# Keys and values of one more batch in three fp32r products, and new orders on all engines, in a fused attention and BitLinear kernel

## What is computed

```python
def xattn(q, ctx, mask):
    Q, K, V = proj(q, wq, bq), proj(ctx, wk, bk), proj(ctx, wv, bv)
    scores = jnp.where(mask == 0, 1e-9, Q @ K.T / sqrt(32))
    return softmax(scores) @ V @ wo + bo

def bitlinear(x, w, b):          # rmsnorm, 8-bit rows of x, ternary w
    return act_quant(rmsnorm(x)) @ weight_quant(w).T + b

x = x + xattn(layernorm(x), ctx, mask)
x = x + bitlinear(gelu(bitlinear(layernorm(x), w1, b1)), w2, b2)
```

## Time and profile before

| what | value |
|---|---|
| median of 3 runs | 652.19 us (651.63 to 652.81) |
| the profiled execution | 650.6 us |
| its span in the trace | 648.8 us |
| granted TensorE clock | 1.00 |
| PE busy | 628.9 us (97%) |
| DVE busy | 574.3 us (89%) |
| ACT busy | 530.2 us (82%) |
| POOL busy | 518.7 us (80%) |

### The profile page before, as it was taken

How to read it: one execution, slowest core, us unless ns; L and a number is a source line. 1 busy time by engine, 2 the same in 40 slices (tenths; PEclk the granted TensorE clock), 3 DMA queues, 4 the chain that set the end, 5 groups by cost and what they waited for, 6 DMA issues and landing times.

```text
span 648.8 us, 14114 instructions
## 1 busy us (share of the span) xinstructions
PE 628.9 (97%) x4904; PEld 423.7 (65%) x4904; DVE 574.3 (89%) x1062; ACT 530.2 (82%) x1450; POOL 518.7 (80%) x653
## 2 busy tenths in 40 slices
PE   8988999999999999999999999999999999999996
PEld 6746886666666676766666676666667666565542
DVE  5697889999999988999899988999889799999894
ACT  2579679987889888887898878888988889998674
POOL 3297977979977898688967899778959778999776
PEclk9999999999999999999999999999999999999999
DMA  8983310424315443354224343043333122543236
GB/s 291 402 300 111 126 41 9 107 45 106 84 28 115 103 91 75 38 135 90 71 67 114 74 121 74 10 132 87 90 74 74 24 75 41 128 86 88 62 61 182
DMA packets 109286, 65.38 MB, mean 101 GB/s; under 512 B 90856, under 2 KB 90856, under 8 KB 108576
## 3 DMA queue, kind: packets, MB, share of 16 engines
q1 hardware_dynamic: 108159, 64.49, 37.9%
q10 hardware_dynamic: 1056, 0.00, 0.1%
HBM read 35.12 MB, written 8.39 MB: 67 GB/s over the span
## 4 chain that ended last, share of the span: by engine, by line
PE 67%; POOL 13%; DVE 8%; DMA 4%; ACT 4%; issue 3%; SPq 0%; POOLq 0%; DVEq 0%; ACTq 0%
PE ps_a L573 23%; PE ps_y L710 11%; PE ps_z L687 11%; PE ps_t L646 6%; PE ps_s L636 4%; PE ps_a L658 3%; POOL hid L2270 2%; POOL prob L2259 2%; DMA q_hT<-q_h 2%; PE ps_y L580 2%; DVE hs L1633 2%; POOL q_h L2275 2%; PE ps_a L607 2%; ACT prob L1145 2%; DMA wk_s<-in_L_xattn_wk_dram 1%
## 5 line engine op out<-in xcount | busy, mean ns | idle before, releaser
L1145 ACT ACTIVATE prob<-ps_s,nmax 128x120 f32<-128x120 f32 x512 | 178.9, 377 | 24.7 <-DVE nmax L1579 19.2
L2259 POOL TENSOR_TENSOR prob<-prob,pinv 128x480 f32<-128x480 f32 x128 | 129.2, 1017 | 41.0 <-DVE pinv L1584 40.0
L687 PE MATMUL ps_z<-w1T,q_xT 128*128 128x512 fp8e4 x476 | 122.8, 380 | 0.5 <-DVE hid L1625 0.4
L1145 ACT ACTIVATION_READ_ACCUMULATOR prob<-ps_s,nmax 128x1 f32 x512 | 113.3, 221 | 0.0
L710 PE MATMUL ps_y<-w2T,q_hT 128*128 128x512 fp8e4 x448 | 105.5, 379 | 1.5 <-DMA q_hT<-q_h 1.5
L1625 DVE SCALAR_TENSOR_TENSOR hid<-ps_z,y_deq,b_row 128x512 f32<-128x512 f32 x119 | 88.0, 739 | 10.6 <-PE ps_z L687 9.2
L1576 DVE COPY_PREDICATED_SCALAR ps_s<-hidden_key,masked_c 128x480 f32 x128 | 90.5, 707 | 4.2 <-PE ps_s L636 3.9
L1121 ACT COPY probT<-ps_t 120x512 f32<-120x512 f32 x128 | 76.9, 601 | 15.4 <-PE ps_t L646 14.3
L1579 DVE TENSOR_REDUCE nmax<-ps_s 128x4 f32<-128x480 f32 x128 | 84.1, 657 | 4.4
L646 PE MATMUL ps_t<-ident,prob 128*120 128x128 f32 x512 | 77.9, 275 | 4.3 <-POOL prob L2259 3.7
L646 PEld LDWEIGHTS ps_t<-ident,prob 128*120 128x120 f32 x512 | 60.0, 137 | 25.3 <-issue 7.4
(11 more groups left out here) (207 smaller groups left out, 1373.7 us busy)
## 6 DMA issues: line engine op xcount, KB each, us to landing
x<-in_x_dram SPq DMA_DIRECT2D x32, 256.0 KB, 2.9
out_dram<-x SPq DMA_DIRECT2D x32, 256.0 KB, 2.8
xn<-in_x_dram SPq DMA_DIRECT2D x7, 1024.0 KB, 6.6
hid<-in_L_ffn_w_dram SPq DMA_DIRECT2D x4, 1024.0 KB, 9.6
ctx_k<-in_ctx_dram SPq DMA_DIRECT2D x8, 240.0 KB, 3.1
ctx_k<-in_mask_Bx1xSxS_ik_dram SPq DMA_DIRECT2D x7, 240.0 KB, 3.1
xn<-in_x_dram SPq DMA_DIRECT2D x4, 256.0 KB, 3.5
x<-in_L_xattn_wq_dram SPq DMA_DIRECT2D x1, 1024.0 KB, 7.3
```

The source lines that it names most:

```text
L687: last = nc.tensor.matmul(bank[:], q_xT[:, k % 3, i], w1T[:, i, c * CH:(c + 1) * CH], start=(i == 0), stop=(i == KD - 1))
L1145: last = nc.scalar.activation(prob[:, n % 3, g * S2:(g + 1) * S2], ps_s[n % HG][:, g * S2:(g + 1) * S2], ACT.Exp, bias=nmax[:, n % 4, g:g ...
L2259: gp.tensor_tensor(pr, pr, pinv[:, n % 4].unsqueeze(2).to_broadcast([P, HG, S2]), ALU.mult).then_inc(s["prob_ready"], 1)
```

## The change

One number changes, `CTX3` from 3 to 2, and the lists of all five engines are written out anew. Nothing else differs: the steps themselves, their buffers and their waits are the same text (the waits that name `CTX3` follow it). The diff has 1848 lines; its core, stretch by stretch:

```diff
-    CTX3 = 3
+    CTX3 = 2
...
             load_wk()
+            load_piece(0)
             load_piece(1)
-            load_piece(0)
+            load_piece(2)
             load_piece(3)
-            load_piece(2)
             load_x(1)
+            load_first_mask()
             load_wo()
-            load_first_mask()
             load_wv()
...
+            load_x(2)
+            load_residual(5)
+            load_mask(1)
             load_residual(1)
```

PE, the start, one loop iteration's first part, and the end:

```diff
             turn_xn(0, 2)
+            turn_xn(0, 3)
             project_ctx(0, "k")
-            turn_xn(0, 3)
-            turn_keys(0)
             first_q(0)
             first_q(1)
             first_q(2)
+            turn_keys(0)
...
             for a in range(2, 6):
                 ffn_up(4 * a - 4, 2)
+                turn_probs(16 * a - 3)
                 scores(4 * a)
                 turn_xn(a + 1, 0)
-                turn_probs(16 * a - 3)
                 ffn_up(4 * a - 4, 3)
+                turn_probs(16 * a - 2)
                 project_out(4 * a - 2)
                 turn_xn(a + 1, 1)
+                turn_probs(16 * a - 1)
                 ffn_up(4 * a - 3, 0)
-                turn_probs(16 * a - 2)
                 project_ctx(a + 1, "k")
                 ffn_up(4 * a - 3, 1)
                 ffn_down(4 * a - 5, 0)
-                turn_probs(16 * a - 1)
                 ffn_down(4 * a - 5, 1)
...
             ffn_up(31, 1)
-            ffn_down(28, 0)
             ffn_up(31, 2)
             ffn_up(31, 3)
+            ffn_down(28, 0)
             ffn_down(28, 1)
```

ACT, the start and the roundings (they stood after `evac_probs(18)` and `evac_probs(24)`):

```diff
+            evac_turn(("x", 0, 3))
             evac_keys(0)
-            evac_turn(("x", 0, 3))
-            evac_q(0, 0)
             sum_abs(0)
             sum_abs(2)
+            evac_q(0, 0)
...
             evac_turn(("x", 1, 3))
+            round_wv()
             evac_probs(5)
+            exps(8)
             evac_q(1, 0)
             evac_piece(4, 0)
+            round_wk()
             evac_probs(6)
```

DVE, the start and the new list from the third tile's maxima to the first up product (the splits stood after `oT_low(5)` and `softmax_max(29)`):

```diff
             sum_abs(1)
+            sum_abs(3)
             add_bk(0)
             scale_bq()
-            sum_abs(3)
             weight_scales(0)
             ln1_stats(1, 0)
             ln1_stats(1, 1)
+            hide(0, mask0_in)
             ln1_stats(1, 2)
             ln1_stats(1, 3)
-            hide(0, mask0_in)
```

DVE, one loop iteration's first part, and the end:

```diff
                 evac_up(4 * a - 4, 2)
+                invert_sums(16 * a - 1)
                 softmax_max(16 * a)
+                evac_up(4 * a - 4, 3)
                 softmax_max(16 * a + 1)
-                invert_sums(16 * a - 1)
-                evac_up(4 * a - 4, 3)
...
             evac_up(30, 0)
-            ln2_scales(31)
             evac_up(30, 1)
             evac_up(30, 2)
+            ln2_scales(31)
             evac_up(30, 3)
             h_scale(29)
```

POOL, the start, the stretch of the w2 pieces and the loop's first part:

```diff
             round_piece(1)
+            ln1_apply((0, 1))
             normalize(0)
             round_piece(2)
             normalize(1)
-            ln1_apply((0, 1))
             ln1_apply((2, 3))
...
             add_bo(0)
+            normalize(6)
             round_piece(5)
-            add_bo(1)
-            normalize(6)
+            round_piece(6)
             normalize(7)
-            round_piece(6)
             round_piece(7)
             normalize(8)
+            add_bo(1)
+            round_piece(4)
             normalize(9)
-            round_piece(4)
...
             for a in range(2, 6):
+                normalize(16 * a - 2)
+                round_x(4 * a - 3)
                 y_factor(4 * a - 3)
-                round_x(4 * a - 3)
-                normalize(16 * a - 2)
+                normalize(16 * a - 1)
                 add_bo(4 * a - 1)
```

More of the change, by code:

```diff
@@ L813, in _ @@
             turn_piece(6, (0, 1))
+            project_q(1, 2)
+            scores(3)
+            turn_piece(6, (2, 3))
             turn_probs(9)
-            project_q(1, 2)
-            turn_piece(6, (2, 3))
-            scores(3)
+            project_out(1)
             turn_piece(7, (0, 1))
             turn_probs(10)
-            project_out(1)
             turn_piece(7, (2, 3))
@@ L1018, in _ @@
             attend(26)
+            scores(28)
             ffn_up(24, 2)
             turn_probs(109)
-            scores(28)
+            project_out(26)
             turn_probs(110)
-            project_out(26)
             ffn_up(24, 3)
+            turn_probs(111)
             ffn_down(22, 0)
-            turn_probs(111)
             ffn_up(25, 0)
@@ L1774, in _ @@
             evac_piece(1, 1)
+            evac_piece(1, 3)
             softmax_max(3)
@@ L1885, in _ @@
             ln1_stats(3, 3)
-            evac_down(0)
-            softmax_max(25)
+            residual(4)
+            ln2_stats(4)
+            evac_up(3, 0)
             softmax_max(26)
-            residual(4)
-            evac_up(3, 0)
+            add_bk(2)
             invert_sums(24)
-            add_bk(2)
-            ln2_stats(4)
+            invert_sums(25)
             softmax_max(27)
-            invert_sums(25)
+            h_scale(2)
+            invert_sums(26)
             ln2_scales(4)
-            h_scale(2)
+            evac_up(3, 1)
             hide(2, mask_in)
-            invert_sums(26)
+            oT_low(5)
             softmax_max(28)
-            evac_up(3, 1)
-            oT_low(5)
-            split_wk()
-            evac_down(1)
             invert_sums(27)
@@ L1978, in _ @@
-                invert_sums(16 * a + 9)
+                invert_sums(16 * a + 8)
+                residual(4 * a)
+                invert_sums(16 * a + 9)
+                ln2_stats(4 * a)
+                ln1_stats(a + 2, 3)
+                evac_up(4 * a - 1, 0)
+                softmax_max(16 * a + 10)
                 softmax_max(16 * a + 11)
-                add_bk(a + 1)
-                evac_up(4 * a - 1, 0)
-                ln1_stats(a + 2, 3)
+                ln2_scales(4 * a)
+                hide(a + 1, mask_in)
@@ L2033, in _ @@
             evac_up(21, 3)
+            xT_low(7, 2)
             softmax_max(101)
+            residual(23)
+            evac_up(22, 0)
             invert_sums(99)
-            xT_low(7, 2)
-            residual(23)
             h_scale(21)
+            add_bv(7)
             invert_sums(100)
-            evac_up(22, 0)
-            add_bv(7)
+            ln2_stats(23)
+            evac_up(22, 1)
             xT_low(7, 3)
-            evac_up(22, 1)
-            ln2_stats(23)
             softmax_max(102)
+            softmax_max(103)
+            invert_sums(101)
             oT_low(24)
+            evac_up(22, 2)
+            evac_down(20)
+            invert_sums(102)
             ln2_scales(23)
-            invert_sums(101)
-            softmax_max(103)
-            evac_up(22, 2)
-            invert_sums(102)
-            evac_down(20)
+            invert_sums(103)
             evac_up(22, 3)
-            invert_sums(103)
+            add_bk(7)
             softmax_max(104)
@@ L2112, in _ @@
             softmax_max(118)
+            softmax_max(119)
+            invert_sums(116)
+            evac_up(26, 0)
+            residual(27)
             evac_down(23)
-            evac_up(26, 0)
-            softmax_max(119)
-            residual(27)
-            invert_sums(116)
             ln2_stats(27)
+            evac_up(26, 1)
             invert_sums(117)
```

789 lines of the change are left out of this document (390 added, 399 removed).

## The result

The median went from 651.33 to **655.42 us** (15 runs each, 653.39 to 657.6 after): ratio 1.006, 95% interval 1.0051 to 1.007. That is slower by 0.6%, 4.1 us, inside the predicted range (649.9 to 656.3), but not the likeliest case (652.9, no change) and above the forecast's own range of 651.4 to 654.4. Two single runs, one of before at 908.49 us and one of `late_splits` at 716.77, lie far above the others of their kernel and are left out where kernels are compared. The profiled execution of after took 653.84 us, span 651.8, 3.0 longer than the span of before; its mean granted clock is 0.997.

What follows compares the result with a forecast made beforehand. PE was taken as the bound, busy 628.9 of 648.8 us, with DVE second. Products -1.3, splits +2.4, start +0.4, relief -0.8, loop and tail zero gave +0.7: median 652.9 us, range 649.9 to 656.3.

Steps and rivals of the forecast that it cites:

- the likeliest case: Whole kernel: terms sum to +0.7 us, median 652.9, no change that counts; chance 0.38.
- Products: Third batch on PE: two fp32 products become three fp32r products each, 3.43 to 2.80 us apiece; -1.3 us.
- Splits: wk's and wv's subtractions move to about 65 to 80 us, overfilling DVE; PE loses +2.4 us, bounds 0.9 and 3.5.
- three places that I had named: From 66 to 96: w2 transposition waits for its bank, query product for the residual, ACT for maxima.
- the one slack of 1.1 at 90.89: The evacuation at 89.17 ends 1.1 us before PE needs its bank; this was set against DVE's 3.5 us overrun.
- Start: First weight sums: last piece now summed on DVE, POOL begins 0.5 us later; +0.4 at PE, bounds 0 and 0.8.
- Relief: Where the splits leave, 142 to 165 us, PE's 0.78 us lost should go; -0.8, bounds 0 and -1.85.
- Loop: Four iterations of 74.4 us without a PE gap can only get worse; forward probability transposition has 1.4 us to spare; zero.
- the rival's mechanism: Loop: scaling for the forward probability transposition slips past its 1.4 us, PE waits four times, 1.0 each; 656.9, chance 0.10.
- The sign I had argued: Loop: with no PE gap in its four iterations, it could only get slower, not faster; size taken as zero.
- Tail: After the loop, end set by tile 29; later up product eats into PE's 1.85 us wait; zero, bound 1.0 either way.
- two held-up splits: Both splits collide with POOL from 65 to 89 us: PE loses 3.5, sum +1.8, 654.0; chance 0.20.

Runs made afterwards that it cites:

- late_splits: The changed kernel with the products of the kernel before (CTX3 = 3) and roundings and splits at their old places; 659.84 us, ratio 1.0143.
- new_tail: The kernel before (CTX3 = 3) with only what follows the loop taken from the changed kernel; 652.23 us, ratio 1.0014.
- old_loads: The changed kernel with the old order of the first loads and of the sums that follow them; 653.98 us, ratio 1.0047.
- h_sooner: The changed kernel with the two roundings of a hidden tile one step sooner on POOL in the loop; 652.81 us, ratio 1.0043.
- tail_apart: h_sooner with one POOL bias addition moved ahead of the rounding of tile 27 in the tail; 654.46 us, ratio 1.0052.
- new_loop: The kernel before (CTX3 = 3) with only the loop's new lists from the changed kernel; 653.61 us, ratio 1.0036.

## Why the range held and the likeliest case did not

*Products: right.* The third batch's products stand in the chain of after at 2.78 and 2.80 us.

```profile
119.17 2.78 PE ps_a L573 x12
...
124.12 2.80 PE ps_a L573 x12
```

*Splits: right mechanism, too dear.* DVE's timeline after:

```profile
24.65 2.29 DVE L1690 TENSOR_REDUCE w_abs<-raw_wv_h 128x1 f32<-128x2048 f32 x1 [3.36 <-DMA raw_wv_h<-in_L_ffn_w_dram]
...
67.70 3.30 DVE L1726 TENSOR_TENSOR wv_l<-wv_s,wv_h 128x2048 fp32r<-128x2048 f32 x1
...
77.89 2.26 DVE L1721 TENSOR_TENSOR wk_l<-wk_s,wk_h 128x2048 fp32r<-128x2048 f32 x1
...
100.53 0.65 DVE L1730 TENSOR_TENSOR ctxT_l<-ps_y,ctxT_h 128x480 fp32r<-128x480 f32 x1
```

3.30 + 2.26 = 5.56 against the 5.7 taken: one held up, one free, as in the earlier trace rows. DVE is full, a bank's evacuation is what PE waits for at 82.72, and the residual at 75.23, two of the three places that I had named. But PE loses 1.33 and not 2.4 from 66 to 96 (bounds 0.9 and 3.5). I set DVE's overrun against the one slack of 1.1 at 90.89; PE's largest wait there is 0.69 for POOL, which both splits held up in turn (POOL's timeline):

```profile
68.96 3.81 POOL L2314 TENSOR_SCALAR hid<-hid 128x2048 f32<-128x2048 f32 x1
...
77.87 3.12 POOL L2260 TENSOR_TENSOR prob<-prob,pinv 128x480 f32<-128x480 f32 x1
```

The same rounding takes 1.91 at 64.88, and such a scaling 0.99: 4.0 us of POOL's time, and POOL's work runs on almost without a break from there to the scaling that PE waits for at 93.27. My sum had no term for POOL.

*Start: size not settled.* The last sum took 2.29, the key bias 0.65, POOL began 0.27 later (28.19 for 27.92, predicted 0.5), and PE's transposition behind POOL's wait comes 0.39 later (53.06 for 52.67), as predicted (+0.4). By tile 2's scores it is 1.1, above the bound of 0.8, with a wait of 0.97 at 61.84, which no step of mine had. But one pair of traces does not measure this: `new_tail`, whose start is that of before line for line, reaches the same two steps at 53.29 and 64.02, since its wk landed later (first product at 14.08 for 13.43). So +0.4 is no proof of the mechanism, and 0.65 of the 1.1 is within what one start differs from itself. In the trace of after the granted clock also fell at 28; but in `old_loads`, where it did not, tile 1's scores come no sooner.

*Relief: half right.* From 142 to 165 PE has no gap (-0.78), and the 0.47 after 225 went to 0.11, which my sum had left out. From 96 to 142 it lost 0.38 more: the wait at 116.86.

*Loop: the step that failed.* "Zero" for the loop was argued for the probability transposition alone; that indeed made no wait, so the rival's mechanism did not happen either. But on POOL the forward scalings stand ahead of the rounding of a hidden tile, and I never followed that rounding through SP's queue to its user, nor the rows of x beside it. With 4.7 us from issue to use for a hidden tile and landings of 4.3 to 6.0, and with 3.4 for a tile of x that landed in 4.0, PE lost 2.39 from 300 to 525, in two waits rather than four of 1.0. The sign I had argued ("can only get worse") was right and its price of zero was not.

*Tail: within its bound in this trace.* PE's waits from 525 on sum to 4.82, for 5.40 before. `new_tail` alone cost 1.2, a little over the bound of 1.0, with the meeting described above.

With the loop's 2.4 in the sum, +0.7 becomes +3.1, against +3.2 of the profiled execution. That it fits so closely is luck: the errors of splits (-1.1), start (+0.7 by this pair of traces) and the rest nearly cancel. So is part of the range's holding: its upper end was set by two held-up splits, a late start and a tail of +1.0, while the loop, which took 2.4 of the 3.2, stood in the sum with zero. **What stays open:** the profiled execution of after is one of its fastest, and 0.9 of the 4.1 by the medians is in no trace. Neither the late landings (`h_sooner` has the spread still) nor the meeting in the tail (`tail_apart`) settles why after's runs spread over 4.2 us.

## What to carry to other kernels

Follow a moved operation to the user behind the DMA, and compare the room from issue to use with the longest landing of its kind in the trace, not with its median: a stretch without a gap says nothing of how much room its transfers have. When a change shifts work of 5.6 us on an engine that is 87% busy, price it by what the other engine loses too: here the two splits cost POOL 4.0 us, and PE's largest wait in that stretch was for POOL. And orders written out by hand are fitted to each other: in most of these runs a part of a new order, or one mended wait, brought a wait at another place.

## What the runs showed of the hardware

*The granted clock fell after a short wait.* Busy time by stage of after, around 28 us:

```profile
26.00:28.00 2.00, 0.96 (x5) 0.90 (x6) 1.93 (x7) 0.33 (x1) 0.00 (x0) 1.00 1.06 385
28.00:30.00 2.00, 2.00 (x7) 1.53 (x7) 1.90 (x7) 1.51 (x3) 1.81 (x1) 0.58 1.05 398
30.00:32.00 2.00, 1.82 (x5) 0.90 (x3) 1.93 (x5) 0.14 (x1) 1.92 (x2) 0.56 1.08 433
32.00:34.00 2.00, 1.31 (x34) 1.23 (x35) 0.03 (x2) 2.00 (x2) 1.65 (x5) 1.00 1.00 407
```

PE had waited 1.65 us for the last sum of the weights just before; then the clock stood close to the lower of its two levels (1.2 of 2.4 GHz) for some 4 us, and successive products started 0.43 us apart instead of 0.23. `new_loop`, with the start of before, shows 0.83 from 40 to 50, after a wait of 1.61. It belongs to neither start, and such a wait doesn't settle it: before and `new_tail` wait 1.62 and 1.61 at the same step and stay at 1.00.
